# The second layer's attention placed inside the next batch of the first gated network, on one core of a Trainium2 chip

## What is computed

```python
x = x + tanh(g_xattn[0]) * L0_xattn(ctx, layernorm(x))     # graph attention
x = x + tanh(g_ffn[0])   * L0_ffn(layernorm(x))            # first gated network
x = x + tanh(g_xattn[1]) * L1_xattn(layernorm(x), ctx)     # layer 2's attention
x = x + tanh(g_ffn[1])   * L1_ffn(layernorm(x))            # layer 2's feed-forward part

def L0_xattn(h, adj):       # per batch, h is the context, adj the normed x
    sim = einsum('bhnd,bhmd->bnm', h @ Wq.T, h @ Wk.T) / (sqrt(32) * 4)
    A = sigmoid(sim) * (sim >= the 153rd largest value of its row)
    return (1 - gamma) * adj + gamma * (A + A.T) / 2
def L0_ffn(x):
    return fwht(silu(x @ W1.T) * (x @ W3.T)) @ W2.T     # 2048 hidden units
def L1_xattn(p, k_v):
    kv = k_v @ W_k.T + b_k
    sim = layernorm((p @ kv) @ kv.T * 512 ** -0.5) * ln_gamma + ln_beta
    return softmax(sim)
```

## Time and profile before

| | us |
|---|---|
| median of 3 runs (4285.64 to 4291.95) | 4287.12 |
| the profiled execution | 4288.03 |
| its span, from first to last instruction | 4285.8 |
| start, to the first projection of batch 2 | 0 to 134.4 |
| graph attention and gated network | 134.4 to 884.6 |
| layer 2's attention | 884.6 to 1021.9 |
| entry of layer 2's feed-forward part | 1021.9 to 1035.7 |
| all behind it | 1035.7 to 4285.8 |

### The profile page before, as it was taken

One profiled execution on the slowest core, in us unless ns is written; L12 is line 12 of the kernel. 1 busy time (PEld: TensorE's weight loads), 2 busy tenths in 40 slices (PEclk: granted clock), 3 DMA queues, 4 the chain that ended last, 5 costly groups with the idle time before them and its releaser, 6 DMA issues.

```text
span 4285.8 us, 37884 instructions
## 1 busy us (share of the span) xinstructions
PE 3719.1 (87%) x11778; PEld 1714.8 (40%) x11779; DVE 1987.1 (46%) x3526; ACT 1372.1 (32%) x2828; POOL 362.7 (8%) x387
## 2 busy tenths in 40 slices
PE   1899898954658999729987999999999998999999
PEld 0344344421324444316653434434434433444444
DVE  8455554145467777311115665665666663111111
ACT  5424331021125666402223434434434432001000
POOL 6000000000012221031111000000000000000000
PEclk6999999977878999869998999999999999999999
DMA  2321121230031222045554110000000001222221
GB/s 91 135 72 59 59 74 64 69 129 3 0 76 49 54 61 52 32 152 162 163 171 140 43 53 34 23 34 33 23 34 34 22 23 49 78 79 88 76 86 54
DMA packets 77518, 292.43 MB, mean 68 GB/s; under 512 B 10440, under 2 KB 11336, under 8 KB 66252
## 3 DMA queue, kind: packets, MB, share of 16 engines
q1 hardware_dynamic: 69072, 265.17, 19.0%
q0 software_dynamic: 8320, 25.71, 2.0%
HBM read 256.73 MB, written 33.59 MB: 68 GB/s over the span
## 4 chain that ended last, share of the span: by engine, by line
PE 61%; issue 25%; DVE 7%; ACT 4%; DMA 2%; POOL 1%; SPq 1%; POOLq 0%; DVEq 0%; ACTq 0%
PE BM L1824 5%; PE BM L344 5%; PE BR L344 5%; PE BM L1875 5%; PE BR L1883 4%; PE BS L1859 3%; PE BT L1153 3%; PE BS L361 3%; PE BT L361 3%; PE BM L1834 2%; PE BR L1510 2%; PE BM L1499 2%; PE BR L1499 2%; PE BT L1868 2%; PE BM L1848 2%
## 5 line engine op out<-in xcount | busy, mean ns | idle before, releaser
L344 PE MATMUL BM<-XT,AR 128*128 (+1 forms) x1024 | 462.3, 594 | 7.1 <-DMA AR<-l_w_dram 4.9
L344 PE MATMUL BR<-XT,AR 128*128 (+1 forms) x1024 | 460.3, 592 | 0.0
L1935 ACT COPY AR<-BM 128x512 f32<-128x512 f32 x340 | 199.5, 587 | 396.5 <-PE BM L1875 185.8
L1941 ACT ACTIVATE AR<-BS,AR 128x512 f32<-128x512 f32 x256 | 175.7, 690 | 411.5 <-DVE AR L2035 411.5
L344 PEld LDWEIGHTS BM<-XT,AR 128*128 128x128 f32 x1024 | 194.8, 191 | 254.2 <-issue 254.2
L344 PEld LDWEIGHTS BR<-XT,AR 128*128 128x128 f32 x1024 | 194.6, 190 | 244.9 <-issue 244.9
L2048 DVE SCALAR_TENSOR_TENSOR X<-BR,AR,X 128x512 f32<-128x512 f32 x256 | 191.9, 750 | 214.0 <-PE BR L1883 204.8
L399 DVE TENSOR_TENSOR AR<-AR,BR 128x512 f32<-128x512 f32 x80 | 55.0, 687 | 473.6 <-PE BR L344 473.6
L2035 DVE TENSOR_REDUCE AR<-BS 128x2 f32<-128x1024 f32 x128 | 156.9, 1226 | 252.5 <-PE BS L1859 252.5
L1883 PE MATMUL BR<-AR 128*128 128x512 f32 x512 | 255.5, 622 | 3.9 <-DVE X L2048 0.3
L1824 PE MATMUL BM<-XT,AR 128*128 128x512 f32 x512 | 236.5, 605 | 1.3 <-ACT XT L240 1.3
(11 more groups left out here) (326 smaller groups left out, 5349.8 us busy)
## 6 DMA issues: line engine op xcount, KB each, us to landing
AR<-l_w_dram SPq DMA_DIRECT2D x128, 512.0 KB, 3.7
AR<-l_wq_dram SPq DMA_DIRECT2D x32, 1152.0 KB, 5.1
AR<-l_w_dram SPq DMA_DIRECT2D x42, 768.0 KB, 4.9
AR<-w2h SPq DMA_DIRECT2D x16, 1024.0 KB, 4.8
QS<-qx SPq DMA_DIRECT2D x32, 512.0 KB, 9.7
AR<-l_w_dram SPq DMA_DIRECT2D x16, 1024.0 KB, 4.8
AR<-l_w_dram SPq DMA_DIRECT2D x8, 1408.0 KB, 17.5
made<-AR SPq DMA_DIRECT2D x40, 256.0 KB, 5.0
```

The source lines that it names most:

```text
L344: last = nc.tensor.matmul(bank.rearrange("p (a n) -> p a n", a=1), w[:, kt, a, :], XT[:, ds(b & 1, 1), kt, :], start=kt == 0, stop=kt == K ...
L1935: nc.scalar.copy(to, BM[:, L3[job] % 2, :]).then_inc(m_free, 1)
```

## The change

It unrolls the work of the first layer over batches and groups (Python loops in place of engine loops), and places in it the attention of layer 2: the attention of batch b - 1 runs inside the network of batch b, that of the last batch behind it. Its norm's transposes come after the first group's units and go to a tile of their own (XT1), the keys after those of the second, the context between the halves of the second down product, the scores after the third group's units; normalisation, maximum, exponentials and addition lie in the fourth group. The projections of the next batch come ahead of a batch's first unit, its similarities behind it; STEPS has the 32 steps in three groups, up to three beside a unit. The graph is turned after the first unit of the fourth group, into S_BANKS, and added beside the second unit; the norm for the next network is made beside the third, its transposes lie ahead of the fourth group's down product. On GpSimd the first norm's root comes ahead of the key operations (`keys_pool`), and the copies of the context (L757) are gone, since TensorE reads CT directly. On SyncE the first up tiles are loaded ahead of the wait for the Hadamard product; the attention's weights are loaded at the network's third group, those of the feed-forward part at its sixth, thirteenth and at the end; of the rows for the entry only the last batch's is fetched after the last addition. The joined memory plan lets all of it lie side by side.

```diff
-STEPS = ((2, 2, 2, 1, 1, 1), (2, 2, 2, 1, 1, 1), (2, 2, 1, 1, 1, 1), (2, 2, 1, 1, 0, 0))
-FOUND_STEP, FOUND_LAST = 5, 7 + ST
+STEPS = ((0, 3, 3, 3, 0, 0), (3, 3, 3, 2, 2, 1), (3, 3, 3, 0, 0, 0), (0, 0, 0, 0, 0, 0))
...
+        def norm_scalar_l1(act):
+            for kt in range(KT):
+                nc.scalar.copy(XT1[:, kt, :], full(act, turn, T_ACT)).then_inc(turn.free, 1)
+

         a = area()
+        CT = a(B * S)
...
+        def l0_sync(sp):
+            f = l0f
+
...
+            for u in range(UG):
+                up(0, u)
+            sp.wait_ge(l0f.m.free, 2 + ST + HAD_M + 2)
+            sp.dma_start(w2h.rearrange("g p n -> p g n"), WH[1].rearrange("p (g u) n -> p g (u n)", u=UG)).then_inc(wh_stored, 16)
+            sp.wait_ge(wh_stored, 16)
+            down(0)
+            for n in range(1, B * ST):
+                b, g = divmod(n - 1, ST)
+                for u in range(UG):
+                    sp.wait_ge(f.r.full, L0["r", b, g, u] + 1)
+                    up(n, u)
+                sp.wait_ge(f.s.full, L0["s", b, g] + ST)
+                down(n)
+                if n == 3:
+                    sp.wait_ge(kx_stored, 32)
+                    sp.dma_start(WK1, l1_wk).then_inc(l1_w, 16)
+                    sp.dma_start(BK1, l1_bk).then_inc(l1_w, 16)
+                    sp.dma_start(BKR, l1_bk_row.to_broadcast([P, C])).then_inc(l1_w, 16)
+                    sp.dma_start(ROWS1, l1_ln.rearrange("(o a) n -> o a n", o=1).to_broadcast([P, 2, S])).then_inc(l1_w, 16)
+                if n == 6:
+                    for dst, src in ((AGG, l1_agg), (D1, l1_d1), (COLS, l1_cols)):
+                        sp.dma_start(dst, src).then_inc(l1f_w, 16)
+                    sp.dma_start(OROWS, l1_rows.rearrange("(o a) n -> o a n", o=1).to_broadcast([P, 2, D])).then_inc(l1f_w, 16)
+                if n == 13:
+                    sp.wait_ge(f.s.free, L0["s", 2, ST - 1] + 2 * ST)
+                    sp.dma_start(D2, l1_d2).then_inc(l1f_w, 16)
...
             def turn_graph(b):
                 pe.wait_ge(graph_ready, b * ST + ST + 1)
+                pe.wait_ge(f.s.free, s.now() + ST)
+                s.step(ST)
                 for j in range(ST):
-                    bank = start_job(pe, l0f.r, r)
                     for i in range(ST):
-                        last = nc.tensor.transpose(bank[:, i * P:(i + 1) * P], GRAPH[:, i, j * P:(j + 1) * P], ID[:, :])
-                    last.then_inc(l0f.r.full, 1)
+                        last = nc.tensor.transpose(S_BANKS[j][:, i * P:(i + 1) * P], GRAPH[:, i, j * P:(j + 1) * P], ID[:, :])
+                    last.then_inc(f.s.full, 1)
...
+            def down(b, g, pair):
+                if pair == 0:
+                    pe.wait_ge(f.down_in, (b * ST + g + 1) * 16)
+                else:
+                    pe.wait_ge(turn.free, T_PE.now() + 2)
+                pe.wait_ge(f.s.free, s.now() + 2)
+                s.step(2)
+                for u in range(UG):
+                    if pair == 0:
+                        pe.wait_ge(f.r.free, freed[u])
+                    for j in range(2):
+                        st = 2 * pair + j
+                        last = nc.tensor.matmul(S_BANKS[st], f.HIDDEN[:, u, st * P:(st + 1) * P], f.DOWN[:, u, :],
+                                                start=u == 0, stop=u == UG - 1)
+                        if u == UG - 1:
+                            last.then_inc(f.s.full, 1)
...
+            def l1_context():
+                pe.wait_ge(turn.free, T_PE.now() + 2)
+                pe.wait_ge(f.r.free, r.now() + 2)
+                bank = start_job(pe, f.m, m)
+                for jt in range(ST):
+                    last = nc.tensor.matmul(bank, KV1[:, jt, :], XT1[:, jt, :], start=jt == 0, stop=jt == ST - 1)
+                last.then_inc(f.m.full, 1)
...
             pe.wait_ge(turn.free, T_PE.now() + 2)
-            ffn_tensor_batch(pe, l0f, m, r, s, n_in, B - 1, l0f.groups - 1)
-            ffn_tensor_batch(pe, l0f, m, r, s, n_in, B - 1, 1, lambda: norm_tensor(pe))
+            for b in range(B):
+                for g in range(ST):
+                    assert g or b == 0 or L0["s", b, g] == s.now()
+                    for u in range(UG):
+                        if g == 0 and u == 0 and b < B - 1:
+                            project(b + 1)
+                        assert L0["r", b, g, u] == r.now()
+                        unit(b, g, u)
+                        if g == 0 and u == 0 and b < B - 1:
+                            similarities()
+                        if g == ST - 1 and u == 0 and b < B - 1:
+                            turn_graph(b + 1)
+                    if g == 0 and b:
+                        norm_tensor(pe)
+                    if g == 0 and b < B - 1:
+                        N_PE.step()
+                    if g == 1 and b:
+                        l1_keys(b - 1)
+                    if g == 2 and b:
+                        l1_scores()
+                    if g == ST - 1:
+                        norm_tensor(pe)
+                        if b == B - 1:
+                            l1_keys(b)
+                    assert L0["s", b, g] == s.now()
+                    down(b, g, 0)
+                    if g == 1 and b:
+                        l1_context()
+                    down(b, g, 1)
+            norm_tensor(pe)
+            l1_context()
+            l1_scores()
...
+            def l1_keys():
+                act.wait_ge(l1_w, 64)
+                nc.scalar.activation(KVT1, full(act, f.m, m), ACT.Identity, bias=BK1).then_inc(f.m.free, 1)
+
+            def l1_context():
+                nc.scalar.copy(OUT1, full(act, f.m, m)).then_inc(f.m.free, 1)
+
...
+                        if b < B - 1:
+                            if g == 0 and u == 0:
+                                similarities(b + 1)
+                            count(STEPS[g][u])
+                    if g == 0 and b:
+                        norm_scalar_l1(act)
+                    if g == 1 and b:
+                        l1_keys()
+                        r.step(2)
+                    if g == 2 and b:
+                        l1_scores(b - 1)
+                    if g == ST - 1:
+                        norm_scalar(act, (b + 1) & 1)
+                        if b == B - 1:
+                            l1_keys()
+                            r.step(2)
+                        if b:
+                            l1_exp(b - 1)
+                    if b < B - 1:
+                        count(STEPS[g][UG])
+                    if g == 1 and b:
+                        l1_context()
+                    if b < B - 1:
+                        count(STEPS[g][UG + 1])
                 tr.step()
-                r.step(ST)
-                norm_scalar(act, (b + 1) & 1)
-            ffn_scalar_batch(act, l0f, m, r)
-            norm_scalar(act, 0)
+            norm_scalar_l1(act)
+            l1_context()
+            l1_scores(B - 1)
+            l1_exp(B - 1)

...
             def add_top(b):
                 v.wait_ge(graph_ready, b * ST + ST + 1)
                 for st in range(ST):
-                    then(nc.vector.scalar_tensor_tensor(out=rows(b, st), in0=GRAPH[:, st, :], scalar=GC[:, 2:3], in1=rows(b, st),
-                                                        op0=ALU.mult, op1=ALU.add))
+                    last = nc.vector.scalar_tensor_tensor(out=rows(b, st), in0=GRAPH[:, st, :], scalar=GC[:, 2:3], in1=rows(b, st),
+                                                          op0=ALU.mult, op1=ALU.add)
+                then(last)

             def add_graph(b):
                 for st in range(ST):
-                    nc.vector.scalar_tensor_tensor(out=rows(b, st), in0=full(v, l0f.r, r), scalar=GC[:, 2:3], in1=rows(b, st),
-                                                   op0=ALU.mult, op1=ALU.add).then_inc(l0f.r.free, 1)
-                v.wait_ge(l0f.r.free, r.now() + 2)
+                    v.wait_ge(f.s.full, s.step())
+                    nc.vector.scalar_tensor_tensor(out=rows(b, st), in0=S_BANKS[st], scalar=GC[:, 2:3], in1=rows(b, st),
+                                                   op0=ALU.mult, op1=ALU.add).then_inc(f.s.free, 1)
+                v.wait_ge(f.s.free, s.now() + 4)
                 v.sem_inc(x_done, 1)

-
...
+            for b in range(B):
+                t = 0
+                if b:
+                    norm_turned(b - 1)
+                if b < B - 1:
+                    m.step(2)
+                for g in range(ST):
+                    for u in range(UG):
+                        v.wait_ge(f.m.free, m.step() + 2)
+                        silu = f.SILU[:, r.bank(), :]
+                        bank = full(v, f.r, r)
+                        nc.vector.tensor_tensor(f.HIDDEN[:, u, :], silu, bank, ALU.mult).then_inc(f.r.free, 1)
+                        if b < B - 1:
+                            if g == 0 and u == 0:
+                                m.step(ST)
```

(73 more changed lines are left out.)

338 lines of the change are left out of this document (142 added, 196 removed).

## The result

The changed kernel takes 4165.19 us (median of four runs, 4161.75 to 4166.46) beside 4286.65 for the kernel before (four runs on the same chip, 4285.64 to 4291.95): ratio 0.9713, 95% interval 0.9696 to 0.973, so 121.5 us less.

What follows compares the result with a forecast made beforehand. TensorE bounds the network, chains through all engines the turns and attention. An attention end 102.2 us earlier plus 5.1 at the next stage's entry gives 107.3 off 4287.1: forecast 4180 us, range 4160 to 4212.

Steps and rivals of the forecast that it cites:

- The bound and the mechanism: Network bound by TensorE, turns and layer 2's attention by chains through all engines; turns pay for three of four attentions.
- Batch by batch: First gated network: TensorE needs 177.9, 198.5, 198.5 and 182.3 us for its four batches, 757.2 in all against 750.2 before.
- The attention's norm: End of group 1, batches 2 and 3: transposes wait for ScalarE behind search steps, clock falls; 11 us together.
- Its keys: Layer 2's attention inside the network: 2 + 8 key instructions on TensorE, 0.9 + 1.7 us.
- The start: Ahead of the network: norm's root before key operations, transposes at 117.7 us, first projection at 121.2 instead of 134.4.
- The tail: Behind the network: batch 4's attention stays exposed, 1.0 + 11.7 + 28.6 us, ending at 919.7 instead of 1021.9.
- The entry: Start of layer 2's feed-forward part: one row of X left to fetch, 2.4 us instead of 7.5, 5.1 gained.
- the fifth: Engine loops replaced by straight code: instruction supply costs 0 to 13 us, taken as 0; no gain booked.
- A: VectorE and ScalarE come late in the network, norms 5 us late in three batches: 4195 to 4215 us; chance 0.22.
- C: Straight code on four engines is fetched late beside weights, slower than before: 4324 us at 3 us a block; chance 0.03.
- D: The weave does not hide the attention's vector work, which adds some 23 us for three batches: 4250 us; chance 0.05.
- B: Clock holds and ScalarE is free sooner, attention norms cost 2.3 to 8 us: 4163 to 4174 us; chance 0.10.

Runs made afterwards that it cites:

- Experiment 7: Changed kernel with graph turn, addition and next norm put back between the batches, layer 2's attention still inside the network: 4206.15 us, ratio 0.9804.
- 5: Changed kernel with GpSimd's two key operations ahead of the first norm's root again: 4180.57 us.
- 6: Changed kernel with all four rows of X and the next stage's small rows loaded only after the last addition again: 4176.81 us.
- experiment 1: Changed kernel with three search steps of the first group's fourth unit moved behind the attention norm's copies: 4153.04 us, ratio 0.9683.
- 8: Changed kernel with up to four search steps beside a unit instead of three, same steps in all: 4193.18 us.
- experiment 9: Kernel before the change with only its engine loops written out as straight code: 4281.76 us beside 4290.85, ratio 0.998.
- 4: Changed kernel with search steps behind the norm, similarity copies ahead of sigmoids, and the last attention's maximum taken tile by tile: 4146.37 us, ratio 0.9664.
- 2: Changed kernel with ScalarE copying all four similarity banks out before taking the sigmoids from the copies: 4160.38 us, one execution.
- experiment 3: Changed kernel with search steps behind the attention norm and similarity copies ahead of sigmoids: 4143.87 us, ratio 0.966; repeated with more rounds 4141.72 us, ratio 0.9652.

## Why the prediction was right, and where it was off

**The bound and the mechanism** held. TensorE bounds the network and the chains through all engines bound the turns and the attention; the weave removes the chains. Experiment 7 puts 36.0 us on the turns, 5 puts 12.9 at the first projection on GpSimd's order, 6 puts 5.7 on the loads. The rest, layer 2's attention, is read from the traces.

**Batch by batch**: forecast 177.9, 198.5, 198.5 and 182.3, measured 178.5, 195.9, 195.2 and 180.2 (to the last matmul, at 868.5). The network came out at 749.8 instead of 757.2. The sizes that were off:
- The attention's norm was put at 11 and measured 10.0 and 9.3: the wait 5.59 (forecast "five to six"), the down product 8.48 and 7.80 instead of 6.87, so the clock took 1.6 and 0.9 where I had booked 2.4.
- Its keys, 2 + 8 instructions, took 1.75 instead of 2.6. I had priced the eight small ones from a row at a mixed clock at 1.7; they take 0.9:

```profile
384.70 1.05 PE L557 MATMUL BR<-AR 128*128 128x128 f32 x8
```

- The graph's turn took 1.75 instead of 2.1. Context and scores, 3.43 and 3.57, were right to 0.05, and the context inside the network did run at the high clock. The next norm with its small wait took 2.6 instead of 2.9.

**The start** came at 118.70 instead of 121.2: the transposes began at 115.55, not 117.7. Before, the Hadamard product ended near 118.6; the transposes that follow it now begin 3.1 us ahead of that, outside the 0 to 2 that I had allowed. The wait of 1.97 us inside the graph's turn is gone, since its four banks fill without one:

```profile
100.55 1.97 PE L441 MATMUL BR<-ID,AR 128*128 128x128 f32 x8 [1.97 <-DVE X L586]
102.31 16.29 PE L450 MATMUL BM<-AR 128*128 128x512 f32 x32
...
98.66 1.91 PE L519 MATMUL BT<-ID,AR 128*128 128x128 f32 x8
100.37 15.34 PE L580 MATMUL BM<-AR 128*128 128x512 f32 x32
```

The first two lines are from before, the last two from the changed kernel. I had most of this gain lost again in the product behind it, "at the low clock for longer". It took 15.34 us instead of 16.29, and 14.82 to 15.81 in experiments 1 to 8; with the loops written out and the wait kept (experiment 9) it took 15.51, so its length also changes without this edit. The transposes behind it ran at the high clock. The key operations cost nothing.

**The tail** took 38.7 instead of 41.3: context at 3.71 and not 5.36, 0.7 in the norm, the rest in shorter waits. **The entry** took 8.06; I had expected 8.7.

**Where the 13.1 us went.** The entry came 13.1 us earlier than forecast: 2.5 at the start, 7.4 in the network, 2.6 in the tail and 0.6 behind it. All the terms erred to the same side, most of all the clock after the attention norm's wait (2.7 with that norm's other rows), the keys (2.5 in three batches) and the start (2.5). That the result still lies in the range says little for the single sizes.

**The step that was argued wrongly** is the fifth, "no loops: I take 0". I bounded the edit between 0 and a loss of 13 and excluded a gain, because no stall shows at the group's turns. That reason covered only the place where TensorE is full. Experiment 9 shows a gain of 5.6 us ahead of the entry, and 9 in the times. But it is not what the forecast lacked: 5.1 us were gained in the turns and 1.4 in the attention's rounds (1.5 were lost ahead of the first unit), and of these stretches the changed kernel has only the last attention left. There the norm, from the last eviction to the context, took 11.0 us instead of the 11.7 of the looped rows, with 0.68 for 1.12 and 7.34 for 7.42 among its waits. Some 0.7 us of that stretch is what the traces put on the loops, the clock's share included.

**The rivals.** A, C and D fell: no wait for VectorE's products, no "issue" gap in the network's straight code, and VectorE carries 21 us more in batches 2 and 3 than in batch 1 (123.8 against 102.4) while TensorE has no wait in the network that is put down to it. The time lies in B's bracket (4163 to 4174), but B's mechanism is refuted: the clock did not hold and ScalarE was not free sooner. The bracket was met by other terms, which is luck for B and no merit of the forecast. It is experiment 1 that shows what B's shorter norms would have given, 12 us on top.

## What to carry to other kernels

Weaving a chain-bound stage into a TensorE-bound one gains the chain's whole length and costs its matmuls and the waits that it brings, as long as each engine's extra work fits under one unit. Count the spare per unit and per engine: here 0.59 us for three steps, and one more step turned it into 27 us. Look then at what stands ahead of the woven copies in each engine's queue, since one wait of 5.6 us was worth 7 with its clock, and moving three small steps behind it gave all of it back. When loops go away, price waits as well as turns. Before a gain of a few us is believed, look whether the same matmuls ran at the same clock in both traces.

## What the runs showed of the hardware

- The same wait was followed by either clock. After 7.3 us of waiting and the same sixteen transposes, the exposed context took 3.71 us in the changed kernel and in experiments 4, 5 and 8, and 5.73 to 5.87 in experiments 1, 2, 6 and 7. With both edits (experiment 3) it took 3.71 in one execution and 6.25 in another of the same kernel. That is 2 to 2.5 us which come or go without an edit.
- A wait of 2.90 us for ScalarE, 1.29 ms behind the entry, was followed by matmuls at 1.00 in the changed kernel and at 0.50 in the first execution of experiment 3, 3.1 us more.
- Unchanged code behind the entry took between 3248.4 and 3256.9 us in the profiled executions of these kernels. Gains below some 5 us need the stage's own trace.
- Most waits in looped code were longer than in straight code, by 0.07 to 0.35 us each, though the loops' bodies ran at the same pace.
- A load of ScalarE's table took 1.28 us, and TensorE waited for it while ScalarE held a bank (1.79 us in the similarities).
